# The bias of the first pair as a rank-one product: three banks filled by TensorE ahead of the data

## The chip, the cores and the metric

One core of one Trainium2 chip runs the whole program. The metric is the device time in microseconds (us) of one execution. The kernel before took 922.59 us, the median of three runs (922.33 to 923.38).

## The reference

`x` has 128 samples of 64 channels by 1024 columns. Each sample is first mixed by a 64x64 matrix that its condition picks out of 16; the result goes through a linear layer with a bias (`W`, `b`) and, beside it, through a low-rank product (`A`, `B`, weighted by `p_scores`) that is clamped against the linear part by row norms.

```python
cond = jnp.einsum('bct,bcd->bdt', x, cond_w[itok])          # 64 x 64 per sample
z = jnp.einsum('bsd,od->bso', cond, W) + b
u = jnp.einsum('bsd,edr->ebsr', cond, A)
m = jnp.einsum('ebsr,ero,e->bso', u, Bm, p_scores)
gamma = jnp.minimum(0.5 * norm(z) / (norm(m) + 1e-6), 1.0)  # norms over the last axis
out = x + z + gamma * m
```

## The kernel before

Two samples fill the 128 partitions and make a tile; there are 64 tiles in 32 pairs (tile r = 0 and r = 1 of a pair). For each tile TensorE mixes the channels by a block-diagonal `mixer` (plain float32 matmuls, `mix`, line 888) into PSUM, ScalarE and VectorE split the result into a high and a low part (`y_hi`, `y_lo`), and TensorE multiplies the parts with the high and low parts of `W` in three passes (`product`, line 901). `W` is cut into four 512x512 blocks W11, W12, W21, W22. Pairs 1 to 31 save products by a Strassen-like scheme, which needs sums of the blocks (T1 to T4, made by VectorE in pair 0) and sums of the tiles' halves (S1 to S4). Pair 0 doesn't: it does all eight block products plainly (`plain`) while the weights still arrive. Its results stand in four banks: z11 in `b_ps`, z21 in `a_ps`, z12 in `c_ps` and z22 in half of `m_ps`. `plain_done` counts them (5 for z11, 6 for z21, 7 for z12, 8 for z22).

Every engine works through its own list in the order of the code, and all waits are semaphores written by hand; no scheduler moves anything. What the change and the prediction touch:

- TensorE's opening: once a tile of zeros is set, `WARM` = 8 bf16 matmuls of 512 columns (line 982) into `u_ps`; then `mix` of tile 0 into `mix_ps` when `x_loaded[0]` and `mixer_loaded[0]` are there, `mix` of tile 1 into `m_ps`, and the plain products.
- ScalarE's opening: it issues the load of the first chunk of W11 (line 504), loads its table (line 506, which releases GpSimd's load of tile 1, line 380), and issues two of the four loads of mixer blocks (lines 509 and 510); SyncE issues the other two (lines 277 and 278).
- SyncE loads the bias, spread over 128 partitions, as the last of the constants (line 287).
- VectorE in pair 0 adds the bias while it takes z11 (line 764), z21 (772), z12 (778) and z22 (784) out of PSUM. Between them stand the making of T3, T1, T2 and T4 (lines 609, 616, 623 and 630), the sum and the low part of `u` (676 and 681), and the low parts of the next pair's `y` (649).
- ScalarE in pair 0, after splitting the weights: `b_hi` (526), the square of z11 (464), a copy of half of `u_ps` (450), `u_hi` (455), then for pair 1 high parts and copies (430 and 436), the square of z12 (471), and high parts of T4 and T2 (425).
- Four waits of TensorE behind it: `up(1)` of pair 0 (line 960) waits for z22; the second product into `b_ps` of pair 1 for VectorE's line 746; the product with S3 for VectorE's line 714; and the mix of tile 5 for VectorE's line 649.

Of the kernel before, what the change touches and what calls it, by code (L numbers as in the profile page):

```python
# [5 lines left out]
def conditioned_clamped_low_rank_linear_kernel(  # L6
# [26 lines left out]
    ALU = mybir.AluOpType  # L33
# [13 lines left out]
    WARM = 8  # L47
    STEPS = PAIRS // 2
    CLAMP, EPS = 0.5, 1e-6
    W11, W21, W22, T1, T2, T3, T4 = range(7)  # L50
    W12 = T4
# [13 lines left out]
    with ctx:  # L65
# [6 lines left out]
        def sem(name):  # L72
            return ctx.enter_context(nc.semaphore(name))
# [16 lines left out]
        bias = sb("bias", [P, 3, H], fp32)  # L90
# [8 lines left out]
        s23 = sb("s23", [P, 2, HC, P], fp32)  # L99
# [19 lines left out]
        idle = squares[:, lo]  # L119
        raw11 = w_hi_raw[:, T1, :, :]  # L120
# [28 lines left out]
        bias_loaded = sem("bias_loaded")  # L149
        idle_set = sem("idle_set")  # L150
# [83 lines left out]
        def y_part(tile, r, h):  # L234
            return tile[:, h * HC:(h + 1) * HC, r * P:(r + 1) * P]
# [23 lines left out]
        def _(sp):  # L259
# [26 lines left out]
            sp.dma_start(b_raw, bm.rearrange("e r o -> (e r) o")).then_inc(bm_loaded, 16)  # L286
            sp.dma_start(bias[:, 0:2, :], b.rearrange("(o h n) -> o h n", o=1, h=2).to_broadcast([P, 2, H])
# [121 lines left out]
        def _(act):  # L409
# [35 lines left out]
            def copy_u(p, first):  # L445

                act.wait_ge(u_done, p + 1)
                if not first:
                    act.wait_ge(m_done[0], p)
                nc.scalar.copy(u_raw[:, :], u_ps[:, 2 * P:4 * P]).then_inc(u_copied, 1)  # L450

            def split_u(p):

                act.wait_ge(u_summed, p + 1)
                nc.scalar.copy(u_hi[:, :], u_raw[:, :]).then_inc(u_hi_ready, 1)

            def square_z11(p, par, opening):

                act.wait_ge(z11_ready, p + 1)
                if not opening:  # L460
                    act.wait_ge(z12_squared, p)
                    act.wait_ge(m_squared[1], p)
                    act.wait_ge(z0_sum_ready, p)
                nc.scalar.activation(squares[:, lo], z0[:, par, lo], ACT.Square,  # L464
                                     accum_out=z11_sq).then_inc(z11_squared, 1)
# [37 lines left out]

            act.dma_start(raw11[:, 0, :], w_blocks[W11][0]).then_inc(w_loaded[W11][0], 16)
# [21 lines left out]
            nc.scalar.copy(b_hi[:, :], b_raw).then_inc(b_hi_ready, 1)  # L526
            square_z11(0, 0, True)
            copy_u(0, True)
            split_u(0)
# [69 lines left out]
        def _(dve):  # L599
# [147 lines left out]

            nc.vector.memset(mixer[:, :, :], 0.0).then_inc(mixer_zeroed, 1)
# [14 lines left out]
            dve.wait_ge(plain_done, 5)  # L763
            nc.vector.tensor_tensor(z0[:, 0, lo], b_ps[:, :], bias[:, 0, :], ALU.add).then_inc(z11_ready, 1)
# [6 lines left out]
            dve.wait_ge(plain_done, 6)  # L771
            nc.vector.tensor_tensor(z1[:, lo], a_ps[:, :], bias[:, 0, :], ALU.add).then_inc(z21_ready, 1)
# [4 lines left out]
            dve.wait_ge(plain_done, 7)  # L777
            nc.vector.tensor_tensor(z0[:, 0, up_], c_ps[:, :], bias[:, 1, :], ALU.add).then_inc(z12_ready, 1)
# [105 lines left out]
        def _(pe):  # L884
# [30 lines left out]
            def plain(bank, r, h, n):  # L915

                product(bank, y_part(y_hi, r, h), y_part(y_lo, r, h), n, h == 0, h == 1, r == 0, True
                        ).then_inc(plain_done, 1)
# [62 lines left out]
            for _ in range(WARM):  # L981
                nc.tensor.matmul(u_ps[:, :], idle[:, 0:P], idle, start=True, stop=True)
            pe.wait_ge(x_loaded[0], 16)
# [10 lines left out]
            for r, bank in ((0, c_ps[:, :]), (1, m_ps[:, lo])):  # L994
                plain(bank, r, 0, W12)
# [13 lines left out]
            plain(m_ps[:, lo], 1, 1, W22)  # L1009
# [104 lines left out]
```

## Time and profile before

| what | value |
|---|---|
| median of 3 runs | 922.59 us |
| time of the profiled execution | 922.25 us |
| its span | 920.3 us |
| mean granted TensorE clock | 0.998 |
| busy: TensorE matmul, weight load | 909.4 us (99%), 772.5 us (84%) |
| busy: VectorE, ScalarE, GpSimd | 589.7 us (64%), 367.6 us (40%), 321.3 us (35%) |
| chain that ended last | TensorE 92%, VectorE 4%, the rest under 2% each |

The chain of waits is on TensorE nearly all the time. Its busy time counts a matmul from its start to the modelled end of its results, so one matmul that follows another closely overlaps it; how far apart two of them start is the better price.

### The profile page before, as it was taken

What the parts mean: (1) busy time and instruction counts of PE and PEld (TensorE: products, weight loads), DVE (VectorE), ACT (ScalarE), POOL (GpSimd) and SP (SyncE); (2) the same over time, 40 slices, a digit from 0 to 9 for tenths busy, and PEclk for the clock granted to TensorE, in tenths of its full rate; (3) what the DMA queues carried; (4) which work ended last, traced back from release to release, by engine and by line L of the source; (5) the groups of instructions that cost most, each with busy time, mean ns of one, the idle gap of its engine ahead of it and who ended that gap; (6) DMA issues with size and microseconds to landing.
All of it is one profiled execution on the core that took longest, in us unless ns stands there. A gap on an engine that the chain in (4) does not pass through costs nothing.

```text
span 920.3 us, 14732 instructions
## 1 busy us (share of the span) xinstructions
PE 909.4 (99%) x4628; PEld 772.5 (84%) x4628; DVE 589.7 (64%) x930; ACT 367.6 (40%) x727; POOL 321.3 (35%) x318
## 2 busy tenths in 40 slices
PE   8999999999999999999999999999999999999997
PEld 6878888888888888888888888888888888888885
DVE  6996666556665666665576656666655757566665
ACT  6653343334334333433343343334333433433342
POOL 0024443234433244332344322443323443224432
PEclk9999999999999999999999999999999999999999
DMA  8212221122221222211222212222112222122211
GB/s 300 74 70 95 72 95 57 60 94 94 71 92 40 78 94 71 94 51 66 94 94 71 88 39 84 94 71 94 47 70 94 94 71 83 37 91 94 73 47 68
DMA packets 32744, 75.16 MB, mean 82 GB/s; under 512 B 12761, under 2 KB 13786, under 8 KB 32730
## 3 DMA queue, kind: packets, MB, share of 16 engines
q1 hardware_dynamic: 32138, 73.91, 22.8%
q10 hardware_dynamic: 448, 0.56, 0.2%
q0 software_dynamic: 144, 0.52, 0.1%
q8 instruction: 7, 0.11, 0.1%
q14 instruction: 7, 0.06, 0.0%
HBM read 41.42 MB, written 33.55 MB: 81 GB/s over the span
## 4 chain that ended last, share of the span: by engine, by line
PE 92%; DVE 4%; issue 1%; SPq 1%; DMA 1%; ACT 0%; POOL 0%; DVEq 0%; POOLq 0%
PE b_ps L901 35%; PE c_ps L901 18%; PE mix_ps L888 11%; PE m_ps L960 9%; PE a_ps L901 9%; PE u_ps L941 6%; PE u_ps L945 3%; DMA a_lo_raw<-in_L_ffn_A_dram 1%; DVE w_lo L640 1%; SPq L271 1%; DVE s_lo L670 0%; DVE y L649 0%; DVE w_lo_raw L616 0%; DVE w_hi_raw L630 0%; DVE w_lo_raw L623 0%
## 5 line engine op out<-in xcount | busy, mean ns | idle before, releaser
L430 ACT CAST y<-mix_ps 128x512 fp32r<-128x512 f32 x126 | 74.4, 591 | 298.5 <-PE mix_ps L888 298.5
L368 POOL TENSOR_TENSOR stats<-stats 128x1 f32<-128x1 f32 x32 | 17.8, 556 | 456.9 <-ACT squares L483 456.9
L901 PE MATMUL b_ps<-w_hi,y 128*128 128x512 f32 x512 | 168.2, 389 | 0.3 <-DVE z L746 0.3
L670 DVE TENSOR_TENSOR s_lo<-s,s_hi 128x512 fp32r<-128x512 f32 x124 | 135.7, 1114 | 4.2
L888 PEld LDWEIGHTS mix_ps<-mixer,x_in 128*128 128x128 f32 x1008 | 121.9, 191 | 7.6 <-issue 2.9
L888 PE MATMUL mix_ps<-mixer,x_in 128*128 128x128 f32 x1008 | 122.8, 275 | 1.3 <-DMA mixer<-in_L_cond_weights_dram 0.9
L443 ACT CAST s_hi<-s 128x512 fp32r<-128x512 f32 x124 | 76.6, 618 | 115.6 <-POOL s L342 93.4
L354 POOL TENSOR_TENSOR z<-z,x_in 128x512 f32<-128x512 f32 x61 | 79.2, 1299 | 113.7 <-ACT squares L464 113.7
L901 PEld LDWEIGHTS b_ps<-w_hi,y 128*128 128x128 f32 x512 | 96.1, 188 | 20.6 <-DVE z L746 0.7
L649 DVE TENSOR_TENSOR y<-mix_ps,y 128x512 fp32r<-128x512 f32 x126 | 86.4, 687 | 41.5 <-ACT s L436 39.5
L901 PE MATMUL b_ps<-w_lo,y 128*128 128x512 f32 x256 | 99.6, 389 | 0.0
L901 PE MATMUL c_ps<-w_hi,s_hi 128*128 128x512 f32 x248 | 99.1, 400 | 0.0
L901 PE MATMUL b_ps<-w_hi,s_hi 128*128 128x512 f32 x248 | 96.6, 390 | 0.3 <-DVE z L714 0.3
L901 PE MATMUL c_ps<-w_lo,s_hi 128*128 128x512 f32 x248 | 96.7, 390 | 0.0
L901 PE MATMUL c_ps<-w_hi,s_lo 128*128 128x512 f32 x248 | 96.6, 389 | 0.0
L901 PE MATMUL b_ps<-w_hi,s_lo 128*128 128x512 f32 x248 | 96.5, 389 | 0.0
L901 PE MATMUL b_ps<-w_lo,s_hi 128*128 128x512 f32 x248 | 96.5, 389 | 0.0
L720 DVE TENSOR_TENSOR z<-b_ps,z 128x512 f32<-128x512 f32 x31 | 21.4, 692 | 106.1 <-PE b_ps L901 106.1
L901 PE MATMUL a_ps<-w_hi,y 128*128 128x512 f32 x264 | 86.6, 389 | 0.0
L348 POOL TENSOR_TENSOR z<-z,x_in 128x1024 f32<-128x1024 f32 x30 | 72.2, 2408 | 0.0
L941 PE MATMUL u_ps<-y,a_hi 128*128 128x512 f32 x256 | 69.3, 392 | 0.0
L741 DVE TENSOR_TENSOR z<-a_ps,bias 128x512 f32<-128x512 f32 x31 | 21.4, 691 | 57.7 <-PE a_ps L901 57.7
(119 smaller groups left out, 1568.5 us busy)
## 6 DMA issues: line engine op xcount, KB each, us to landing
x_in<-in_x_dram SPq DMA_DIRECT2D x63, 512.0 KB, 3.7
out_dram<-z SPq DMA_DIRECT2D x62, 512.0 KB, 2.8
w_lo_raw<-in_L_ffn_W_dram SPq DMA_DIRECT2D x8, 256.0 KB, 6.3
mixer<-in_L_cond_weights_dram SPq DMA_DIRECT2D x126, 16.0 KB, 2.1
w_hi_raw<-in_L_ffn_W_dram SPq DMA_DIRECT2D x7, 256.0 KB, 6.2
out_dram<-z SPq DMA_DIRECT2D x3, 256.0 KB, 2.0
x_in<-in_x_dram POOLq DMA_DIRECT2D x1, 512.0 KB, 4.0
a_lo_raw<-in_L_ffn_A_dram SPq DMA_DIRECT2D x1, 512.0 KB, 8.1
```

The lines of the kernel that those rows point to most:

```text
L348: nc.gpsimd.tensor_tensor(z1[:, :], z1[:, :], x_in[:, slot, :], ALU.add).then_inc(residual1_ready, 1)
L354: nc.gpsimd.tensor_tensor(z0[:, par, cols], z0[:, par, cols], x_in[:, 2 * par, cols], ALU.add).then_inc(residual0_ready, 1)
L430: nc.scalar.copy(y_part(y_hi, r, h), source(h)).then_inc(y_hi_ready, 1)
L443: nc.scalar.copy(s_hi[:, n, :, :], s_raw(n)).then_inc(s_hi_ready, 1)
L649: nc.vector.tensor_tensor(y_part(y_lo, r, h), source(h), y_part(y_hi, r, h).bitcast(fp32), ALU.subtract).then_inc(y_lo_ready, 1)
L670: nc.vector.tensor_tensor(s_lo[:, n, :, :], s_raw(n), s_hi[:, n, :, :].bitcast(fp32), ALU.subtract).then_inc(s_lo_ready, 1)
L720: nc.vector.tensor_tensor(z1[:, up_], b_ps[:, :], z0[:, par, up_], ALU.add).then_inc(u3_ready, 1)
L888: made = nc.tensor.matmul(source(h)[:, k, :], x_in[:, slot, (h * HC + k) * P:(h * HC + k + 1) * P], mixer[:, r, :], start=True, stop=True)
L901: summed = nc.tensor.matmul(bank, left[:, k, :], right[:, n, k, :], start=(start and k == 0 and i == 0), stop=(stop and k == HC - 1 and i ...
L941: return nc.tensor.matmul(u_ps[:, :], a_hi[:, k, :], y[:, k, :, :], start=(k == 0), stop=(k == KC - 1))
L945: nc.tensor.matmul(u_ps[:, 0:2 * P], a_lo[:, k, :], y[:, k, 0, :], start=False, stop=False)
L960: summed = nc.tensor.matmul(m[:, c], left[:, part], right[:, c], start=(n == 0), stop=(n == 2))
```

## The change

TensorE writes the bias into the three banks `b_ps`, `a_ps` and `c_ps` before the data is there: a matmul of a row of ones (1 partition by 128) with a row of the bias (1 by 512) puts the same row on all 128 partitions. Pair 0's products into these banks no longer begin with a cleared bank but add to it; ScalarE copies z11, z21 and z12 out, where VectorE added the bias. z22 (in `m_ps`) is handled as before. Five of the eight warm-up matmuls go. ScalarE's queue issues a small load of the bias (one partition) as its first act; SyncE's load of the spread bias, which writes over that row, waits until the three matmuls are through. VectorE sets the ones in a part of `s23` that is free then.

```diff
-    WARM = 8
+    WARM = 3
+        ones = s23[0:1, 0, 0, :]
 @sync
+            sp.wait_ge(bias_spread, 3)
             sp.dma_start(bias[:, 0:2, :], b.rearrange("(o h n) -> o h n", o=1, h=2).to_broadcast([P, 2, H])
                          ).then_inc(bias_loaded, 16)
 @scalar
+            act.dma_start(bias[0:1, 0:2, :], b.rearrange("(o h n) -> o h n", o=1, h=2)).then_inc(bias_row_loaded, 16)
             act.dma_start(raw11[:, 0, :], w_blocks[W11][0]).then_inc(w_loaded[W11][0], 16)
...
             nc.scalar.copy(b_hi[:, :], b_raw).then_inc(b_hi_ready, 1)
+            act.wait_ge(plain_done, 5)
+            nc.scalar.copy(z0[:, 0, lo], b_ps[:, :]).then_inc(z11_ready, 1)
             square_z11(0, 0, True)
+            act.wait_ge(plain_done, 6)
+            nc.scalar.copy(z1[:, lo], a_ps[:, :]).then_inc(z21_ready, 1)
             copy_u(0, True)
+            act.wait_ge(plain_done, 7)
+            nc.scalar.copy(z0[:, 0, up_], c_ps[:, :]).then_inc(z12_ready, 1)
             split_u(0)
 @vector
+            nc.vector.memset(ones, 1.0).then_inc(ones_set, 1)
             nc.vector.memset(mixer[:, :, :], 0.0).then_inc(mixer_zeroed, 1)
...
-            dve.wait_ge(plain_done, 5)
-            nc.vector.tensor_tensor(z0[:, 0, lo], b_ps[:, :], bias[:, 0, :], ALU.add).then_inc(z11_ready, 1)
...
-            dve.wait_ge(plain_done, 6)
-            nc.vector.tensor_tensor(z1[:, lo], a_ps[:, :], bias[:, 0, :], ALU.add).then_inc(z21_ready, 1)
...
-            dve.wait_ge(plain_done, 7)
-            nc.vector.tensor_tensor(z0[:, 0, up_], c_ps[:, :], bias[:, 1, :], ALU.add).then_inc(z12_ready, 1)
 @tensor
-            def plain(bank, r, h, n):
-                product(bank, y_part(y_hi, r, h), y_part(y_lo, r, h), n, h == 0, h == 1, r == 0, True
+            def plain(bank, r, h, n, on_bias=True):
+                product(bank, y_part(y_hi, r, h), y_part(y_lo, r, h), n, h == 0 and not on_bias, h == 1, r == 0, True
                         ).then_inc(plain_done, 1)
...
             for _ in range(WARM):
                 nc.tensor.matmul(u_ps[:, :], idle[:, 0:P], idle, start=True, stop=True)
+            pe.wait_ge(ones_set, 1)
+            pe.wait_ge(bias_row_loaded, 16)
+            for bank, o in ((b_ps, 0), (a_ps, 0), (c_ps, 1)):
+                nc.tensor.matmul(bank[:, :], ones, bias[0:1, o, :], start=True, stop=False).then_inc(bias_spread, 1)
             pe.wait_ge(x_loaded[0], 16)
```

On TensorE, at the start of its list, before:

```order
1 L982 MATMUL u_ps<-squares 128x512 [waits idle_set]
2 L982 MATMUL u_ps<-squares 128x512 x7
3 L888 MATMUL mix_ps<-mixer,x_in 128x128 [waits mixer_loaded0,x_loaded0]
4 L888 MATMUL mix_ps<-mixer,x_in 128x128 x7
5 L888 MATMUL m_ps<-mixer,x_in 128x128 [waits mixer_loaded1,x1_loaded]
```

and of the change (its line numbers are some higher; `s` is the tile with the ones):

```order
1 L989 MATMUL u_ps<-squares 128x512 [waits idle_set]
2 L989 MATMUL u_ps<-squares 128x512 x2
3 L994 MATMUL b_ps<-bias,s 128x512 [waits bias_row_loaded,ones_set]
4 L994 MATMUL a_ps<-bias,s 128x512
5 L994 MATMUL c_ps<-bias,s 128x512
6 L895 MATMUL mix_ps<-mixer,x_in 128x128 [waits mixer_loaded0,x_loaded0]
7 L895 MATMUL mix_ps<-mixer,x_in 128x128 x7
```

Three float32 matmuls of 512 columns stand where five bf16 ones stood, and they wait for a load.

On VectorE, from the making of T3 to that of T4 in pair 0, before:

```order
10 L609 TENSOR_TENSOR w_lo_raw<-w_lo_raw 128x1024 x2
11 L764 TENSOR_TENSOR z<-b_ps,bias 128x512 [waits plain_done,bias_loaded]
12 L766 TENSOR_TENSOR b_lo<-b_lo_raw,b_hi 128x1024 [waits b_hi_ready]
13 L616 TENSOR_TENSOR w_lo_raw<-w_lo_raw,w_hi_raw 128x1024 [waits w_lo_ready,t3_made] x2
14 L769 TENSOR_TENSOR bias<-bias 128x512
15 L772 TENSOR_TENSOR z<-a_ps,bias 128x512 [waits plain_done]
16 L623 TENSOR_TENSOR w_lo_raw<-w_lo_raw 128x1024 [waits w_lo_ready,t1_made]
17 L676 TENSOR_TENSOR u_raw<-u_ps,u_raw 128x256 [waits u_copied]
18 L623 TENSOR_TENSOR w_lo_raw<-w_lo_raw 128x1024 [waits w_lo_ready,t1_made]
19 L681 TENSOR_TENSOR u_lo<-u_raw,u_hi 128x256 [waits u_hi_ready]
20 L778 TENSOR_TENSOR z<-c_ps,bias 128x512 [waits plain_done]
21 L630 TENSOR_TENSOR w_hi_raw<-w_hi_raw,w_lo_raw 128x1024 [waits w_lo_ready,t2_made]
```

and of the change:

```order
11 L621 TENSOR_TENSOR w_lo_raw<-w_lo_raw 128x1024 x2
12 L777 TENSOR_TENSOR b_lo<-b_lo_raw,b_hi 128x1024 [waits b_hi_ready,bias_loaded]
13 L628 TENSOR_TENSOR w_lo_raw<-w_lo_raw,w_hi_raw 128x1024 [waits w_lo_ready,t3_made] x2
14 L780 TENSOR_TENSOR bias<-bias 128x512
15 L635 TENSOR_TENSOR w_lo_raw<-w_lo_raw 128x1024 [waits w_lo_ready,t1_made]
16 L688 TENSOR_TENSOR u_raw<-u_ps,u_raw 128x256 [waits u_copied]
17 L635 TENSOR_TENSOR w_lo_raw<-w_lo_raw 128x1024 [waits w_lo_ready,t1_made]
18 L693 TENSOR_TENSOR u_lo<-u_raw,u_hi 128x256 [waits u_hi_ready]
19 L642 TENSOR_TENSOR w_hi_raw<-w_hi_raw,w_lo_raw 128x1024 [waits w_lo_ready,t2_made]
```

Three additions of 128x512 are gone, two ahead of `u_lo` and one behind it.

On ScalarE, of the change, from `b_hi` to the first high part of pair 1; lines 534, 537 and 540 are new, and the other rows are in their order of before:

```order
33 L532 CAST b_hi<-b_lo_raw 128x1024 [waits bm_scaled]
34 L534 COPY z<-b_ps 128x512 [waits plain_done]
35 L469 ACTIVATE squares,stats<-z 128x512 [waits z11_ready]
36 L537 COPY z<-a_ps 128x512 [waits plain_done]
37 L455 COPY u_raw<-u_ps 128x256 [waits u_done]
38 L540 COPY z<-c_ps 128x512 [waits plain_done]
39 L460 CAST u_hi<-u_raw 128x256 [waits u_summed]
40 L435 CAST y<-mix_ps 128x4x128 [waits mix_done]
```

The copy of z12 stands ahead of `u_hi`.

## Rows read from the trace of the kernel before

**Rows 1.** Page, busy time of the whole span

```profile
PE 909.4 (99%) x4628; PEld 772.5 (84%) x4628; DVE 589.7 (64%) x930; ACT 367.6 (40%) x727; POOL 321.3 (35%) x318
```

**Rows 2.** Waits of TensorE: who waited, for whom, total, times, longest

```profile
PE mix_ps L888 <- DMA mixer<-in_L_cond_weights_dram: 0.9, 1, 0.9
PE mix_ps L888 <- DVE y L649: 0.4, 1, 0.4
PE b_ps L901 <- DVE z L714: 0.3, 1, 0.3
PE m_ps L960 <- DVE z L784: 0.3, 1, 0.3
PE b_ps L901 <- DVE z L746: 0.3, 1, 0.3
```

**Rows 3.** Windows: length, busy PE, PEld, DVE, ACT, POOL, granted clock, DMA

```profile
1.70:5.40 3.70, 3.59 (x8) 1.04 (x8) 0.00 (x0) 1.51 (x3) 0.71 (x2) 1.00 0.70 250
...
66.00:892.00 826.00, 826.00 (x4228) 705.65 (x4227) 517.42 (x826) 321.84 (x649) 305.53 (x298) 1.00 0.22 76
```

**Rows 4.** Timeline, TensorE's opening: start us, busy us, what

```profile
1.73 3.59 PE L982 MATMUL u_ps<-squares 128*128 128x512 bf16 x8 [1.73 <-POOL squares L375]
...
6.18 2.02 PE L888 MATMUL mix_ps<-mixer,x_in 128*128 128x128 f32 x16 [0.86 <-DMA mixer<-in_L_cond_weights_dram]
...
8.25 1.86 PEld L888 LDWEIGHTS m_ps<-mixer,x_in 128*128 128x128 f32 x16 [0.24 <-issue]
```

**Rows 5.** Timeline, TensorE, a mix between products at 32 us

```profile
32.02 1.95 PE L888 MATMUL mix_ps<-mixer,x_in 128*128 128x128 f32 x16
33.72 0.48 PE L901 MATMUL m_ps<-w_hi,y 128*128 128x512 f32 x1
```

**Rows 6.** Timeline, the queues' opening

```profile
0.74 0.40 ACTq L504 DMA_DIRECT2D w_hi_raw<-in_L_ffn_W_dram  x1
...
2.97 0.58 ACTq L509 DMA_DIRECT2D mixer<-in_L_cond_weights_dram  x1
...
3.29 0.71 POOL L380 DMA_DIRECT2D x_in<-in_x_dram  x1 [1.58 <-ACT stats L506]
...
4.40 0.47 SPq L278 DMA_DIRECT2D mixer<-in_L_cond_weights_dram  x1
```

**Rows 7.** Chain of waits, a small load in the opening

```profile
0.72 1.27 DMA cond_ids<-in_itok_B_dram
```

**Rows 8.** Issue to landing of lines 504, 278 and 380, in this order

```profile
DMA to landing us min/median/max: 2.8/2.8/2.8
DMA to landing us min/median/max: 3.8/3.8/3.8
DMA to landing us min/median/max: 4.0/4.0/4.0
```

**Rows 9.** Waits of VectorE from 22 to 66 us, the whole answer

```profile
DVE a_lo L759 <- ACT a_hi L521: 1.5, 1, 1.5
```

**Rows 10.** Timeline of VectorE, pair 0

```profile
33.75 0.42 DVE L681 TENSOR_TENSOR u_lo<-u_raw,u_hi 128x256 fp32r<-128x256 f32 x1
...
34.09 0.68 DVE L778 TENSOR_TENSOR z<-c_ps,bias 128x512 f32<-128x512 f32 x1
...
34.69 1.22 DVE L630 TENSOR_TENSOR w_hi_raw<-w_hi_raw,w_lo_raw 128x1024 f32<-128x1024 f32 x1
```

**Rows 11.** Timeline of TensorE and ScalarE around `u_hi`

```profile
31.79 0.39 PE L901 MATMUL c_ps<-w_hi,y 128*128 128x512 f32 x1
...
32.73 0.41 ACT L455 CAST u_hi<-u_raw 128x256 fp32r<-128x256 f32 x1 [2.87 <-DVE u_raw L676]
...
33.59 0.59 ACT L436 COPY s<-mix_ps 128x512 f32<-128x512 f32 x1
...
34.06 0.60 ACT L430 CAST y<-mix_ps 128x512 fp32r<-128x512 f32 x1
```

**Rows 12.** Timeline, the last wait of TensorE for VectorE

```profile
64.89 2.02 PE L888 MATMUL mix_ps<-mixer,x_in 128*128 128x128 f32 x16 [0.43 <-DVE y L649]
```

More of the change, by code:

```diff
@@ L149, in conditioned_clamped_low_rank_linear_kernel @@
         bias_loaded = sem("bias_loaded")
+        bias_row_loaded = sem("bias_row_loaded")
+        ones_set = sem("ones_set")
+        bias_spread = sem("bias_spread")
         idle_set = sem("idle_set")
@@ L993, in _ @@
                 plain(bank, r, 0, W11)
-            for r, bank in ((0, c_ps[:, :]), (1, m_ps[:, lo])):
-                plain(bank, r, 0, W12)
+            plain(c_ps[:, :], 0, 0, W12)
+            plain(m_ps[:, lo], 1, 0, W12, False)
             for r, bank in ((0, b_ps[:, :]), (1, a_ps[:, :])):
@@ L1008, in _ @@
                 mix(0, 2, h)
-            plain(m_ps[:, lo], 1, 1, W22)
+            plain(m_ps[:, lo], 1, 1, W22, False)
             mix_next_1(0, 0, 0)
```

## The prediction

> **What bounds the kernel now.** I read the busy times first: TensorE's matmuls fill 99% of the span [rows 1]. The windows then show where the other 1% is. From 66 to 892 us TensorE is busy for all of 826.00 us [rows 3], so nothing that pair 0 saves or loses there is made up or lost again: a time by which TensorE is earlier or later at 66 us goes through to the end, one for one. The waits of TensorE are five that bear on this change: 0.9 us for the mixer blocks in the opening, and four of 0.3 to 0.4 us for VectorE, all before 66 us [rows 2]; the last of them is the mix at 64.89 [rows 12]. VectorE in turn waits only once from 22 to 66 us, 1.5 us ahead of `a_lo`, which stands before all that the change touches in pair 0 [rows 9]: behind it VectorE is a full queue, and the four waits are waits for that queue. So two numbers decide: how much later TensorE gets through its opening (call it d), and how much earlier VectorE's queue runs at 64 us.
>
> **The opening: warm-up and spread.** The eight bf16 matmuls take 3.59 us from 1.73 [rows 4]. 512 columns at 1.2 GHz are 0.427 us; eight are 3.42, and the 0.17 left is the tail that every matmul row has (0.39 for 512 columns [rows 11], of which 0.213 at 2.4 GHz). So all eight ran at the lower clock, although the window's granted clock says 1.00 [rows 3]; I trust the spacing. Three of them end at 1.73 + 3 x 0.427 = 3.01.
>
> The row of the bias is issued at 0.74, where the load of W11 was [rows 6]. No row shows this load; the nearest are a 0.5 KB one that lands 1.27 us after its issue [rows 7] and the 256 KB one with 2.8 [rows 8]. That gives 2.0 to 3.5; it is nearer to the small one, so I take it that it doesn't hold TensorE: start at 3.05, by the upper bound 3.54.
>
> The price of one spreading matmul: float32 matmuls are two records each (a mix has 8 in the code and 16 in the trace). Sixteen records of 128 columns start and end within 33.72 - 32.02 = 1.70 us [rows 5], 0.106 each, which is 2 x 128 columns at 2.4 GHz. If the records pass their columns twice, one of 512 columns is 0.427 us at 2.4 GHz and 0.853 at 1.2. The other reading is that loading the weights sets the 0.106 and the columns go through once: then 0.213 and 0.427. I take the first: 6 records x 0.427 or 0.853. The Trainium skill, FP8 and Floating Point Precision, section TensorE Precision Notes, says that true float32 takes four passes through the array: two records of two passes, with which the 1.70 us agree. By the other reading the result would be that of the second case below.
>
> When does the clock rise? Before, the eighth matmul still streamed slowly, until 5.15, and the mix at 6.18 was fast (2.02 us for 16 records, against 3.4 at 1.2 GHz) [rows 4]. So it rose between 5.15 and 6.18, and I take the middle, 5.65. With it: (5.65 - 3.05) / 0.853 = 3.05 records slow, 2.95 x 0.427 = 1.26 us fast, end at 6.91. The first mix then starts 6.91 - 6.18 = 0.73 us later. Ends of this: rise at 5.15 and start at 3.0 give 6.64 (+0.46); rise at 6.18 and start at 3.54 give 7.42 (+1.24).
>
> Part of it comes back at once. The second mix began at 8.25 after 0.24 us in which nothing was issued [rows 4]: line 278's mixer block, issued at 4.40, took 3.8 us, to 8.20 [rows 6, 8]. SyncE's queue isn't moved, so a later TensorE no longer meets this wait: d = 0.73 - 0.25 = 0.5 (0.2 to 1.0).
>
> ScalarE's own queue is 0.40 us later by the new issue [rows 6]: line 509 (2.97), its table, and with the table GpSimd's load of tile 1 (3.29 to 3.7, landing 4.0 later at 7.7 [rows 6, 8], before the second mix wants it). TensorE, busy until 6.9, hides these; were the spread short, they would cost 0 to 0.4. The memset of ones (128 elements on one partition) stands ahead of the mixer's, for which the loads of lines 277 and 509 wait; they wait for the conditions as well, until 1.99 [rows 7], and were issued at 2.97 and later. No row shows it; it is far under the 0.6 us for which a 128x512 addition holds VectorE [rows 10], so it is hidden. SyncE's new wait stands where the queue comes at 16.5 us, long after the spread: nothing. Accumulating onto a bank instead of clearing it changes no column: nothing, and no row suggests a gain.
>
> **Pair 0: three additions leave VectorE, three copies go to ScalarE.** An addition of 128x512 holds VectorE for 34.69 - 34.09 = 0.60 us [rows 10]; three are 1.8 us, and with a full queue all behind would be 1.8 us earlier. But `u_lo` stands among them. It waits for `u_hi`, and ScalarE now makes `u_hi` behind the copy of z12, which waits for the last product into `c_ps`. Its last matmul ended at 31.79 + 0.39 = 32.18 [rows 11], now 32.68; copy at 32.73, `u_hi` one pitch later (34.06 - 33.59 = 0.47 [rows 11]) at 33.20, ending 33.61, `u_lo` at 33.7. Before, it was at 33.75 [rows 10]. So the 1.2 us won ahead of it are spent waiting there, and only the third addition, right behind it, is a gain: T4 starts at 34.04 instead of 34.69, VectorE 0.6 us earlier. This depends on d: VectorE's lead is 1.1 - d.
>
> Behind that, ScalarE's high parts come some 0.5 us later than before (the first at 33.6), which the making of T4 (1.22 [rows 10]) covers; the squares of z11 and z21 have slack, for their users stand behind line 784.
>
> **The four waits.** VectorE is 0.6 us earlier at each. TensorE starts 0.5 us late, loses that against the first (z22) and the second (line 746), whose waits it no longer has, and then meets VectorE's queue again: at the product with S3 and at the mix of 64.89 it is as early as VectorE is. The waits don't vanish, they move by 0.6 us. Sum: VectorE's three additions -1.8, the new wait for `u_hi` +1.2, net -0.6 us at 66 us; the later opening is already paid out of the waits. The profiled execution had a span of 920.3 and a time of 922.25 us: that gives 919.7 and 921.65. The median of the runs lies 0.34 above that execution, so I forecast 922.59 - 0.6 = **922.0 us**. By the bounds of d the gain is 0.1 to 0.9.
>
> **The other cases.** A change of 0.2% is 1.85 us, about what a measurement of this kernel can tell from none; below 920.75 I call it faster, above 924.45 slower.
>
> - Cheap spread (8%). If a record passes its columns once, the spread ends by 5.6 even at the lower clock, d is about 0, the lead of VectorE is 1.1 us, and the time 921.5. For it: weight loading could set the 0.106. Against: 16 records match two passes to the nanosecond. Even with the whole 1.8 us it would be 920.8.
> - The lead doesn't come through (10%). The clock rises later, or ScalarE, which is 0.5 us later at the high parts, keeps VectorE waiting again at the low parts of `y`. With all six records slow the spread ends at 3.05 + 5.12 = 8.17, d is 1.7, and the net +0.6: 922.6 to 923.4. For it: the rise is known only to 1 us.
> - Slower: the spread doesn't count as work (12%). Its matmuls use one of 128 partitions of the array. If they don't raise the clock, the spread ends at 8.17, the mix starts slow, and the rise comes, if as long after the start of the work as before (at least 5.15 - 1.73 = 3.4), at 11.6 or later: 3.4 / 0.213 = 16 records slow, 16 fast (1.7): 13.3 instead of 10.0 for the first product, d = 3.3, and the net 3.3 - 1.1 = +2.2: 924.8 us, and more if the rise is a microsecond later. It decides where d passes 3.0. For it: nothing in the trace shows such a matmul. Against: the rise came after a stretch with no more than these weights and zeros going through. The Trainium skill, TensorE: Matmul & The Clock Gate, Part 4, says that transposes on TensorE are not counted as busy in the same way and leave the clock low; no run here shows such a kind. If it held for one-partition matmuls the time would be that 924.8.
>
> **Chances.** The forecast 70%, the others as given. Faster by over 0.2%: 3% (none of the cases gives it; it is what I leave for a price that I misread). Slower: 11%. Same: 86%. The range is 921.0 to 923.8: it holds the forecast, the cheap spread and the lead lost, and leaves the slow clock out.
>
> **What would show it.** In the profile after: three float32 matmuls in six records from about 3.0, with the first slow (0.85 apart) and the last fast (0.43); first mix at 6.6 to 7.4, without a wait for the mixer; no unissued 0.24 us ahead of the second mix; `u_lo` near 33.7 with VectorE now waiting for `u_hi` some 1 us; T4's making at 34.0; no wait of TensorE for z22 and line 746; waits for lines 714 and 649 still there, the mix of 64.89 at 64.3; 66 to 890 us full. I am wrong if the mix of 64.89 moves by over 1 us either way, if the mix after the spread is slow, or if TensorE waits anywhere else.

## The result, and the profile after

The change takes 925.23 us (median of 12 runs) against 922.82 for the kernel before (12 runs): a ratio of 1.0027, 95% interval 1.002 to 1.0035. It is slower, by 2.4 us, and my 922.0 and range to 923.8 missed it. One of the twelve runs took 1629 us at a mean granted clock of 0.68 and doesn't enter the ratio; the other eleven lie between 924.83 and 926.17. The case to which I gave 12%, at 924.8 us, is what happened. The profiled execution of the change has a span of 922.9 us where before had 920.3.

TensorE's opening in the profile of the change (timeline; start us, busy us, what):

```profile
1.73 1.46 PE L989 MATMUL u_ps<-squares 128*128 128x512 bf16 x3 [1.73 <-POOL squares L380]
...
3.12 2.07 PE L994 MATMUL b_ps<-bias,s 1*128 1x512 f32 x2
...
4.99 1.91 PE L994 MATMUL a_ps<-bias,s 1*128 1x512 f32 x2
4.99 0.33 PEld L994 LDWEIGHTS a_ps<-bias,s 1*128 1x128 f32 x1 [0.52 <-issue]
...
5.84 0.33 PEld L994 LDWEIGHTS c_ps<-bias,s 1*128 1x128 f32 x1 [0.52 <-issue]
...
6.70 1.91 PE L994 MATMUL c_ps<-bias,s 1*128 1x512 f32 x2
...
8.54 3.74 PE L895 MATMUL mix_ps<-mixer,x_in 128*128 128x128 f32 x16
...
12.11 1.95 PE L895 MATMUL m_ps<-mixer,x_in 128*128 128x128 f32 x16
13.82 0.48 PE L908 MATMUL b_ps<-w_hi,y 128*128 128x512 f32 x1
```

The weight loads at 4.99 and 5.84 and the matmuls at 4.99 and 6.70 give the pace of the records: 0.85 us each, 1024 columns at 1.2 GHz. All six are that slow. The first mix starts at 8.54 instead of 6.18 (+2.36), and runs slow itself: 3.57 us until the second mix, where before had 2.11 (8.29 - 6.18, the start in the timeline of before; +1.46). The second mix is fast. The first product starts at 13.82; before it was 10.06. Together d = 3.76 us where I had forecast 0.5. The granted clock in the windows says 1.00 here too:

```profile
1.70:5.40 3.70, 3.67 (x6) 1.45 (x7) 0.00 (x0) 1.79 (x3) 0.71 (x2) 1.00 0.72 230
```

The waits that TensorE still has behind its opening, those of VectorE from 14 to 70 us, then `u_lo` and T4 (VectorE) and the mix of tile 5:

```profile
PE mix_ps L895 <- DVE y L661: 0.4, 1, 0.4
PE b_ps L908 <- DVE z L726: 0.3, 1, 0.3
```

```profile
DVE u_lo L693 <- ACT u_hi L460: 1.7, 1, 1.7
DVE u_raw L688 <- ACT u_raw L455: 1.2, 1, 1.2
```

```profile
36.87 0.42 DVE L693 TENSOR_TENSOR u_lo<-u_raw,u_hi 128x256 fp32r<-128x256 f32 x1 [1.68 <-ACT u_hi L460]
37.21 1.22 DVE L642 TENSOR_TENSOR w_hi_raw<-w_hi_raw,w_lo_raw 128x1024 f32<-128x1024 f32 x1
...
67.47 2.02 PE L895 MATMUL mix_ps<-mixer,x_in 128*128 128x128 f32 x16 [0.43 <-DVE y L661]
```

Of the five waits of [rows 2] the mixer's, z22's and line 746's are gone; those for lines 714 (726 now) and 649 (661) are as long as before. The mix of tile 5 starts 67.47 - 64.89 = 2.58 us later [rows 12], which is the 2.6 us of the spans: nothing behind it matters. So of the 3.76 us lost in the opening, 1.18 did not arrive.

Two questions follow. Why did the clock stay low, and does the move of the additions give back those 1.18 us?

### The profile page after: what moved, and what is told of

It reads as the page before. It is cut to its first block, busy times and chain, and to the rows that moved or that the text cites. A ratio compares the mean times of both kernels' runs of the same rounds, so it can differ in the third digit from the quotient of the medians.

```text
span 922.9 us, 14737 instructions
## 1 busy us (share of the span) xinstructions
PE 913.5 (99%) x4629; PEld 775.3 (84%) x4629; DVE 587.1 (64%) x928; ACT 367.6 (40%) x730; POOL 321.2 (35%) x318
## 4 chain that ended last, share of the span: by engine, by line
PE 95%; DVE 3%; issue 1%; POOL 0%; ACT 0%; DVEq 0%; POOLq 0%
PE b_ps L908 36%; PE c_ps L908 18%; PE mix_ps L895 12%; PE a_ps L908 9%; PE m_ps L967 9%; PE u_ps L948 6%; PE u_ps L952 3%; DVE w_lo L652 1%; DVE s_lo L682 0%; PE m_ps L908 0%; PE b_ps L994 0%; DVE y L661 0%; PE m_ps L895 0%; PE a_ps L994 0%; PE c_ps L994 0%
## 5 line engine op out<-in xcount | busy, mean ns | idle before, releaser
L732 DVE TENSOR_TENSOR z<-b_ps,z 128x512 f32<-128x512 f32 x31 | 21.4, 692 | 106.1 <-PE b_ps L908 106.1
L908 PEld LDWEIGHTS a_ps<-w_hi,y 128*128 128x128 f32 x264 | 49.6, 188 | 10.3
```

The lines of the kernel that those rows point to most:

```text
L732: nc.vector.tensor_tensor(z1[:, up_], b_ps[:, :], z0[:, par, up_], ALU.add).then_inc(u3_ready, 1)
L908: summed = nc.tensor.matmul(bank, left[:, k, :], right[:, n, k, :], start=(start and k == 0 and i == 0), stop=(stop and k == HC - 1 and i ...
```

## Experiments

### Does a matmul of one partition raise the clock?

Three kernels built on the one before, and the change with more warm-up.

```diff
 e1_warm_one_row, on before
-                nc.tensor.matmul(u_ps[:, :], idle[:, 0:P], idle, start=True, stop=True)
+                nc.tensor.matmul(u_ps[:, :], squares[0:1, 0:P], squares[0:1, lo], start=True, stop=True)
```

> The kernel before, whose eight warm-up matmuls read one partition of the zeros in place of 128; same columns, same number, same type. Theory A (matmuls that use one partition of the array don't raise TensorE's clock): the mix at 6.18 runs at 1.2 GHz, 16 records 0.213 us apart instead of 0.117, and the first product starts at 11.5 to 13.5 instead of 10.06; the time is 1 to 2.5 us over that of before. Theory B (float32 matmuls, or their spacing, don't count, the partitions play no part): the mix is fast as before, first product at 10.06, time of before within 0.3 us. Theory C (eight of the bf16 matmuls are needed and the three of the change were too few): as B, fast.

```diff
 e2_float32_all_rows, on before
-    WARM = 8
+    WARM = 3
+            idle32 = squares[:, :].bitcast(fp32)
+            for _ in range(3):
+                nc.tensor.matmul(u_ps[:, :], idle32[:, 0:P], idle32, start=True, stop=True)
```

> The kernel before with three bf16 warm-up matmuls and behind them three float32 ones of 512 columns over all 128 partitions of zeros (as long as the spread of the bias, but no bias and no wait). Theory A: they count; the clock rises between 5.1 and 6.2 us, the last records are 0.43 apart, the first mix starts at 6.6 to 7.2 and is fast, first product at 10.3 to 11.0; time +0.2 to +1 us over before. Theory B: all six records 0.853 apart, first mix at 8.2 to 8.5 and slow, first product at 13.8 as in the change. Theory C: as B.

```diff
 e3_three_warm, on before
-    WARM = 8
+    WARM = 3
```

> The kernel before with three warm-up matmuls in place of eight and nothing behind them. Theories A and C: from 3.0 us on nothing counts, as in the change, so the mix at 6.18 is slow (0.213), the clock rises at 9.5 to 12 and the first product starts at 11.5 to 13.5; time +1 to +3 us. If the clock had risen in the change by its own (a rise that falls at a fixed time, whatever TensorE does), the mix would be fast and the time that of before.

```diff
 e4_eight_warm_and_spread, on the change
-    WARM = 3
+    WARM = 8
```

> The change with eight warm-up matmuls in place of three; the spread of the bias starts at 5.15 instead of 3.12. Theory A: the eight have raised the clock by 6.2, so of the six records one or two are slow and the rest 0.43 apart; end at 7.9 to 8.3, first mix fast, first product at 11.6 to 12.0 instead of 13.82, time 922.8 to 923.8. Theory B, the same if a high clock outlives the float32 records. If one-partition matmuls count as idle and let the clock fall again at once, the mix is slow and the time 925 or more.

The openings of TensorE, first of the eight one-partition warm-ups:

```profile
1.73 3.59 PE L982 MATMUL u_ps<-squares 1*128 1x512 bf16 x8 [1.73 <-POOL squares L375]
5.84 3.75 PE L888 MATMUL mix_ps<-mixer,x_in 128*128 128x128 f32 x16 [0.53 <-DMA mixer<-in_L_cond_weights_dram]
9.39 2.09 PE L888 MATMUL m_ps<-mixer,x_in 128*128 128x128 f32 x16
11.23 0.48 PE L901 MATMUL b_ps<-w_hi,y 128*128 128x512 f32 x1
```

then of the float32 ones over all partitions:

```profile
2.98 4.56 PE L985 MATMUL u_ps<-squares 128*128 128x512 f32 x6
7.37 1.95 PE L888 MATMUL mix_ps<-mixer,x_in 128*128 128x128 f32 x16
9.16 1.95 PE L888 MATMUL m_ps<-mixer,x_in 128*128 128x128 f32 x16
10.86 0.48 PE L901 MATMUL b_ps<-w_hi,y 128*128 128x512 f32 x1
```

and of the change with eight warm-ups:

```profile
5.25 2.07 PE L994 MATMUL b_ps<-bias,s 1*128 1x512 f32 x2
7.12 1.91 PE L994 MATMUL a_ps<-bias,s 1*128 1x512 f32 x2
8.83 1.91 PE L994 MATMUL c_ps<-bias,s 1*128 1x512 f32 x2
10.67 3.60 PE L895 MATMUL mix_ps<-mixer,x_in 128*128 128x128 f32 x16
...
15.81 0.48 PE L908 MATMUL b_ps<-w_hi,y 128*128 128x512 f32 x1
```

In e1, with the same columns and times but one partition instead of 128, the mix is slow (3.55 us from one mix to the next), where before had it fast. In e2 float32 matmuls over all partitions, of zeros, raise the clock on the way: six records take 4.4 us instead of 5.4, and the mix behind them is fast (1.79 from one to the next). So float32 records of this length don't by themselves keep the clock low (against theory B), and three bf16 warm-ups are not too few (against C). What is left is the one partition (A).

Each of the two is one execution, and e1 by itself proves little: in e10 (below) the mix is slow behind eight full-width warm-ups too. The repeated runs carry more. The profiles of the change (924.83 us or more in eleven runs) and of e8 below, which has the same opening (924.59 or more in nine), have a time that is 857.5 to 857.6 us more than the start of the mix of tile 5, and that start 53.7 us behind the first product. By this estimate the first product came at 13.3 us or later in all twenty; with a fast first mix it would have come near 12.1 (8.54 + 2 x 1.78), and earlier still had the clock risen within the spread. And in all six profiles with one-partition matmuls ahead of the first mix (the change, e1, e4, e7, e8, e11) that mix is slow, while in the seven with full-width work alone and more than three matmuls it is fast in five (before, e2, e6, e9, e12), partly slow in e5 and slow in e10. e2 and the change still differ in the values (zeros, against ones and the bias) and in the banks written; e1, with zeros into one bank, is the only kernel that sets this apart.

With nothing behind three warm-ups (e3) the first product started at 12.35, with the spread behind them at 13.82: as far as the clock goes the spread was no better than idling, and it moved the first mix from 5.96 to 8.54. Eight warm-ups ahead of it (e4) did not help: I expected one or two slow records, and all six are slow and the mix too, first product 15.81, time 927.12 us. So the clock had not risen by 10.67 although the eight were through at 5.2, as in before, where a mix at 6.18 was fast. The one-partition records behind them are what differs, or the luck of that run: with eight full warm-ups and nothing behind them the first mix was also partly slow in e5 and slow in e10. One run can't tell these apart.

The times of e1 and e3, 922.43 and 923.39 (922.36 for before on the same chip), are 0.1 and 1.0 us over it, where I expected 1 to 2.5 and 1 to 3: e1 misses, e3 is at the lower bound. e1's first product (11.23) is a little ahead of the expected 11.5 to 13.5 as well, and e2's first mix (7.37) a little behind 6.6 to 7.2. The first products of e1 and e3 are 1.17 and 2.29 us late, and less than half of it arrives at the end. Theory A had the clock right, and I had overlooked what absorbs a late opening.

### Where do the additions' 1.8 us go?

The opening of the change put alone into before (spread done, its result overwritten, VectorE adds the bias as before); and the change with the copy of z12 behind `u_hi`.

```diff
 e8_opening_alone, on before
-    WARM = 8
+    WARM = 3
...
+            sp.wait_ge(bias_spread, 3)               # ahead of the load of the spread bias
...
+            act.dma_start(bias[0:1, 0:2, :], b.rearrange("(o h n) -> o h n", o=1, h=2)).then_inc(bias_row_loaded, 16)
...
+            nc.vector.memset(ones, 1.0).then_inc(ones_set, 1)
...
+            pe.wait_ge(ones_set, 1)
+            pe.wait_ge(bias_row_loaded, 16)
+            for bank, o in ((b_ps, 0), (a_ps, 0), (c_ps, 1)):
+                nc.tensor.matmul(bank[:, :], ones, bias[0:1, o, :], start=True, stop=True).then_inc(bias_spread, 1)
```

> The opening of the change alone: three warm-up matmuls, the load of the bias row, the one-partition spread in float32. Its result isn't used: the products clear their banks as before and VectorE adds the bias as before. Theory D (the moved additions bring nothing here, since VectorE waits for what TensorE, late by the opening, lets ScalarE copy of pair 1): first product at 13.8 as in the change, mix of tile 5 at 67.3 to 67.6 as there (67.47), time 924.9 to 925.5. Theory E (the opening costs 3.7 us and the moved additions give 1.1 back): mix of tile 5 at 68.3 to 68.7, time 926.0 to 926.5.

```diff
 e7_z12_behind_u_hi, on the change
-            act.wait_ge(plain_done, 7)
-            nc.scalar.copy(z0[:, 0, up_], c_ps[:, :]).then_inc(z12_ready, 1)
             split_u(0)
+            act.wait_ge(plain_done, 7)
+            nc.scalar.copy(z0[:, 0, up_], c_ps[:, :]).then_inc(z12_ready, 1)
```

> The change with ScalarE's copy of z12 behind u_hi instead of ahead of it. Theory D (what holds VectorE is the copy of the second half of pair 1's tile, for which the low part of y waits): u_lo at about 35.1 instead of 36.87, the first part of T4 at 35.5 instead of 37.21, but the second part at 39.5 to 39.7 and the mix of tile 5 at 67.3 to 67.6, unmoved. Theory F (the wait for u_hi is what holds it, as I had worked out): the second part of T4 0.5 to 1.2 us earlier and the mix of tile 5 at 66.3 to 67.0.

The opening alone: 925.03 us (9 runs), ratio 1.0025 (1.0015 to 1.0035), the same as the whole change. Its first product was at 14.29 (the clock rose in the second mix), and the mix of tile 5 at 67.98, 53.69 us behind it. In the change it is 67.47 - 13.82 = 53.65, in e7 and e11, which have the same opening and the moved additions, 53.69. The three moved additions bring nothing here: theory E falls.

With z12 behind `u_hi` (925.14 us) `u_lo` comes at 35.18 and T4 at 35.52, 1.7 us earlier than in the change, and then VectorE waits for the copies of pair 1 instead. Its timeline and waits:

```profile
35.18 0.42 DVE L693 TENSOR_TENSOR u_lo<-u_raw,u_hi 128x256 fp32r<-128x256 f32 x1
35.52 1.22 DVE L642 TENSOR_TENSOR w_hi_raw<-w_hi_raw,w_lo_raw 128x1024 f32<-128x1024 f32 x1
...
38.09 0.69 DVE L661 TENSOR_TENSOR y<-mix_ps,y 128x512 fp32r<-128x512 f32 x1 [1.36 <-ACT s L441]
...
39.07 0.69 DVE L661 TENSOR_TENSOR y<-mix_ps,y 128x512 fp32r<-128x512 f32 x1 [0.29 <-ACT s L441]
...
39.68 1.22 DVE L642 TENSOR_TENSOR w_hi_raw<-w_hi_raw,w_lo_raw 128x1024 f32<-128x1024 f32 x1
...
67.56 2.02 PE L895 MATMUL mix_ps<-mixer,x_in 128*128 128x128 f32 x16 [0.43 <-DVE y L661]
```

The second half of T4 is at 39.68 (39.60 in the change) and the mix of tile 5 at 67.56. The wait for `u_hi`, on which I had built my sum, is not what holds VectorE (theory F falls): the low part of `y` needs ScalarE's copy of the mixed tile of pair 1, and that comes when TensorE has mixed it, a fixed time behind the first product.

The start of `a_lo` in before, and the operation to which the text comes back at the end:

```profile
22.53 1.23 DVE L759 TENSOR_TENSOR a_lo<-a_lo_raw,a_hi 128x1024 fp32r<-128x1024 f32 x1 [1.47 <-ACT a_hi L521]
...
54.52 2.39 DVE L670 TENSOR_TENSOR s_lo<-s,s_hi 128x512 fp32r<-128x512 f32 x2
```

The kernels side by side, P the start of the first product, A the start of `a_lo`, M that of the mix of tile 5, all from the timelines:

| kernel | P | A | M | M - P | M - A |
|---|---|---|---|---|---|
| before | 10.06 | 22.53 | 64.89 | 54.83 | 42.36 |
| e1 one-partition warm-up | 11.23 | 22.74 | 65.10 | 53.87 | 42.36 |
| e2 float32 warm-up | 10.86 | 23.32 | 65.68 | 54.82 | 42.36 |
| e3 three warm-ups | 12.35 | 23.14 | 66.04 | 53.69 | 42.90 |
| the change | 13.82 | 23.76 | 67.47 | 53.65 | 43.71 |
| e4 change, eight warm-ups | 15.81 | 25.76 | 69.50 | 53.69 | 43.74 |
| e7 z12 behind `u_hi` | 13.87 | 23.80 | 67.56 | 53.69 | 43.76 |
| e8 opening alone | 14.29 | 23.81 | 67.98 | 53.69 | 44.17 |

Up to here M is the later of P + 53.69 and A + 42.36. In before the second decides, as in e1 and e2, whose P differ and whose M - A is the same 42.36: the load of A lands at 21.4 us, VectorE waits for it, and from there its queue is full to 64. TensorE's opening had 64.89 - 53.69 - 10.06 = 1.14 us to spare. That is what absorbed e1's late product, and what absorbed 1.2 of the 3.76 us of the change. The additions lie on the other of the two paths.

### Is there a version that gains?

If the rule holds, the additions pay once TensorE's opening is cheap. The spread as float32r is one record per matmul (ScalarE rounds the row and the ones; the bias is rounded to float32r for three of pair 0's four blocks), placed behind the first mix, with eight warm-ups. SyncE's load of the spread bias now waits for ScalarE's rounding of the row.

```diff
 e5_cheap_spread_z12_late and e6_cheap_spread, on the change
-    WARM = 3
+    WARM = 8
...
-        ones = s23[0:1, 0, 0, :]
+        ones = s_hi[0:1, 0, 0, :]
+        bias_row = b_hi[0:1, :]
...
+            nc.scalar.copy(bias_row, bias[0:1, 0:2, :].rearrange("p h n -> p (h n)")).then_inc(bias_row_split, 1)
+            act.wait_ge(raw_ones_set, 1)
+            nc.scalar.activation(ones, s23[0:1, 0, 0, :], ACT.Copy).then_inc(ones_set, 1)
...
-            for bank, o in ((b_ps, 0), (a_ps, 0), (c_ps, 1)):
-                nc.tensor.matmul(bank[:, :], ones, bias[0:1, o, :], start=True, stop=False).then_inc(bias_spread, 1)
             pe.wait_ge(x_loaded[0], 16)
             pe.wait_ge(mixer_loaded[0], 16 * PER)
             for h in range(2):
                 mix(0, 0, h)
+            pe.wait_ge(ones_set, 1)
+            pe.wait_ge(bias_row_split, 1)
+            for bank, o in ((b_ps, lo), (a_ps, lo), (c_ps, up_)):
+                nc.tensor.matmul(bank[:, :], ones, bias_row[:, o], start=True, stop=False)
 e5 alone: ScalarE's copy of z12 behind split_u(0), as in e7
```

> The change with a cheap spread: eight warm-up matmuls as before, and the spread behind the first mix, at the high clock, as float32r with one record per matmul (ScalarE rounds the row and the ones first; the bias is rounded to float32r for three of pair 0's four blocks). ScalarE's copy of z12 stands behind u_hi. If the price is three records of 0.21 to 0.23 less the 0.25 us for which TensorE stood ahead of the second mix, the first product starts 0.3 to 0.5 us later than before (10.4 to 10.6 where the load of A lands as before). Theory D: the mix of tile 5 is 0.7 to 0.8 us earlier than before relative to the landing of A, time 921.7 to 922.2. Theory F: with z12 late all 1.8 us of the three additions come through, mix 1.6 to 1.8 us earlier, time 920.7 to 921.2. Theory G (the mix of tile 5 is set by the landing of A alone, the additions don't matter): as before.

> As the cheap spread, but with ScalarE's copy of z12 ahead of u_hi, as in the change. Theory D: mix of tile 5 0.6 to 0.7 us earlier than before, within 0.2 us of the version with z12 late. Theory F: 0.6 to 0.7 us earlier, but the version with z12 late gains 1 us more.

Of e6, the opening of TensorE, ScalarE's high parts of W11, a stall in the first product, and the mix of tile 5:

```profile
5.59 2.02 PE L902 MATMUL mix_ps<-mixer,x_in 128*128 128x128 f32 x16 [0.38 <-DMA mixer<-in_L_cond_weights_dram]
7.54 0.49 PE L1004 MATMUL b_ps<-b_hi,s_hi 1*128 1x512 f32 x1
7.88 0.39 PE L1004 MATMUL a_ps<-b_hi,s_hi 1*128 1x512 f32 x1
8.12 0.38 PE L1004 MATMUL c_ps<-b_hi,s_hi 1*128 1x512 f32 x1
8.43 2.05 PE L902 MATMUL m_ps<-mixer,x_in 128*128 128x128 f32 x16
10.24 0.48 PE L915 MATMUL b_ps<-w_hi,y 128*128 128x512 f32 x1
...
10.58 1.26 ACT L422 CAST w_hi<-w_hi_raw 128x512 fp32r<-128x512 f32 x2 [0.96 <-DMA w_hi_raw<-in_L_ffn_W_dram]
...
12.07 0.47 PE L915 MATMUL b_ps<-w_hi,y 128*128 128x512 f32 x1 [0.19 <-DVE w_lo L623]
...
64.42 2.02 PE L902 MATMUL mix_ps<-mixer,x_in 128*128 128x128 f32 x16 [0.43 <-DVE y L668]
```

Here the load of A was late (`a_lo` at 23.84), and M - A is 64.42 - 23.84 = 40.58, 1.78 less than the 42.36 of before. The path from A can't be longer than that, so it is shorter by at least 1.78: this is the 3 x 0.60 of the additions, in full, and with z12 ahead of `u_hi`. M - P is 54.18 in both, so P decided in both. It is 0.49 over 53.69, of which 0.45 lie in the first product: it stalls for a low part of `W`, behind a chunk of W11 for which ScalarE waits until 10.58 in e6 and 12.06 in e5 (its three in before start at 8.82 without a wait). It is a load that is late, and whether the new work in the opening makes it so isn't shown; the landing of A, too, is latest in these two. In e5 the first mix was partly slow as well (P = 11.03), and M = 65.21. Of the expectations, theory D gave 0.6 to 0.8 us relative to A's landing, and measured are 0.92 and 1.78; F expected z12 late to be the better by 1 us; M - P is the same in both, and e6 has the whole gain without it. Times: 922.38 us (10 runs), ratio 0.9993 (0.9983 to 1.0002) for e5, 922.02 for the single run of e6.

```diff
 e9_spread_in_gaps, on e5
-    WARM = 8
+    WARM = 9
...
+            act.wait_ge(plain_done, 1)               # ahead of b_hi, in whose place the rounded row stands
...
+            nc.tensor.matmul(b_ps[:, :], ones, bias_row[:, lo], start=True, stop=False)      # between the mixes
...
+            def spread_rest():                                                             # ahead of chunk 2 of the first product
+                for bank, o in ((a_ps, lo), (c_ps, up_)):
+                    nc.tensor.matmul(bank[:, :], ones, bias_row[:, o], start=True, stop=False)
```

> The cheap float32r spread with nine warm-up matmuls, the matmul into the first bank between the two mixes and those into the other two within the first product, where the last version had lost 0.2 to 0.5 us waiting for the low parts of W; ScalarE copies z12 behind u_hi. Theory D: first product at about 10.1 to 10.2, no stall in it, but 0.45 us of spread; by the rule the mix of tile 5 at 64.2 to 64.5, time 921.8 to 922.4, a gain of 0.3 to 0.8 us. Rival: one-partition matmuls in the middle of full ones let the clock fall; then the products behind them would be 0.43 apart instead of 0.23 and the time 923.5 or more.

It measured 922.38 us (11 runs), 0.9998 (0.9989 to 1.0007), P = 10.00, M = 64.52, without a low clock behind the one-partition matmuls. The first product took 3.68 us up to the start of the next, 0.84 more than the 2.84 of before (12.90 - 10.06), where I had allowed 0.45; P + 53.69 + 0.84 = 64.53 is its M. So M was just outside the expected 64.2 to 64.5 and no gain can be told from none.

The other path can be shortened without any spread: VectorE makes T3 while it waits for A.

```diff
 e10_t3_ahead_of_a_lo on before; e11_change_t3_ahead on the change
+            make_t3(0)
+            make_t3(1)
             dve.wait_ge(a_hi_ready, 1)
             nc.vector.tensor_tensor(a_lo[:, :, :], a_raw, a_hi[:, :, :].bitcast(fp32), ALU.subtract).then_inc(a_lo_ready, 1)
-            make_t3(0)
-            make_t3(1)
```

> The kernel before with one swap on VectorE: T3 is made ahead of a_lo, for which VectorE stood waiting 1.5 us (for the load of A) while it could have made T3. Theory D, as a rule: the mix of tile 5 starts at the later of (first product + 53.69) and (a_lo + 42.36); in before the second, 64.89. The swap takes about 1.5 us from the second, so the first decides: with the first product near 10.06 the mix starts at 63.7 to 64.0 and the time falls by 0.9 to 1.2 us (0.10 to 0.13%). If the first product starts late in that run (the clock rising later, as in two runs of this study), the gain is less by as much over 11.2. Theory H (TensorE's opening sets the end in before too): nothing moves, 922.6 to 922.9.

> The change with the same swap. Theory D: nothing, since the first product at 13.8 decides: mix of tile 5 at 67.4 to 67.6, time 925.0 to 925.4. Theory H and any theory by which VectorE's queue still decides: 1 to 1.5 us less.

On the change it did nothing, as the rule has it: 924.99 us, P = 13.71, M = 67.40, 53.69 apart. On before the result was 922.98 us (11 runs), 0.9998 (0.9989 to 1.0007), against the expected 0.10 to 0.13% less. The profile shows why in that execution:

```profile
1.73 3.60 PE L982 MATMUL u_ps<-squares 128*128 128x512 bf16 x8 [1.73 <-POOL squares L375]
6.97 3.68 PE L888 MATMUL mix_ps<-mixer,x_in 128*128 128x128 f32 x16 [1.65 <-DMA mixer<-in_L_cond_weights_dram]
10.49 1.95 PE L888 MATMUL m_ps<-mixer,x_in 128*128 128x128 f32 x16
12.19 0.48 PE L901 MATMUL b_ps<-w_hi,y 128*128 128x512 f32 x1
...
65.87 2.02 PE L888 MATMUL mix_ps<-mixer,x_in 128*128 128x128 f32 x16 [0.47 <-DVE y L649]
```

The same eight warm-ups as in before, and the mix slow, at 6.97: P = 12.19, M = P + 53.68. So in this execution P decides. The expectation named this case, but the rule was not put to the test by it. That P had decided in before too (theory H) doesn't fit its M - P of 54.83; the unmoved median alone would. The eleven times of e10 run from 921.35 to 923.70, five of them at 922.2 or less.

```diff
 e12_swap_and_eleven_warm, on e10
-    WARM = 8
+    WARM = 11
```

> The kernel before with T3 made ahead of a_lo and eleven full warm-up matmuls in place of eight. The swap alone gave two groups of times, 921.4 to 921.8 and 922.2 to 923.7; by theory D they are runs in which the clock rose ahead of the first mix and runs in which it rose within it. If so, full work up to 6.4 us, where TensorE now stands idle from 5.2, leaves the first group alone: first product at 10.0 to 10.7, mix of tile 5 at 63.7 to 64.4, all times within 921.2 to 922.2, median 921.5 to 921.9 (0.08 to 0.12% under before). Rival: the two groups come from the loads (the mixer blocks landed 0.8 us later in the profiled run of the swap), and they stay: times from 921.4 to 923.7, median as before.

```profile
1.73 4.12 PE L982 MATMUL u_ps<-squares 128*128 128x512 bf16 x11 [1.73 <-POOL squares L375]
5.87 2.02 PE L888 MATMUL mix_ps<-mixer,x_in 128*128 128x128 f32 x16
8.68 2.02 PE L888 MATMUL m_ps<-mixer,x_in 128*128 128x128 f32 x16 [0.78 <-DMA mixer<-in_L_cond_weights_dram]
10.45 0.47 PE L901 MATMUL b_ps<-w_hi,y 128*128 128x512 f32 x1
...
63.58 2.02 PE L888 MATMUL mix_ps<-mixer,x_in 128*128 128x128 f32 x16
```

This has the lowest median of all, 921.69 us against 922.67 (11 and 15 runs), and the group above 922.4 is gone; but the ratio on record is 0.9993 (it is not the ratio of the medians, 0.9989) with an interval of 0.9984 to 1.0002, so a gain isn't shown. Before spread from 921.3 to 923.7 in the same comparison. M is 63.58, 53.13 behind P, 0.56 less than the rule's 53.69. Two rows of VectorE and one of GpSimd say what the rule lacks:

```profile
25.55 0.69 DVE L764 TENSOR_TENSOR z<-b_ps,bias 128x512 f32<-128x512 f32 x1 [0.85 <-DMA bias<-in_L_ffn_b_dram]
...
53.93 4.38 POOL L354 TENSOR_TENSOR z<-z,x_in 128x512 f32<-128x512 f32 x1 [6.41 <-ACT squares L464]
...
54.14 1.29 DVE L670 TENSOR_TENSOR s_lo<-s,s_hi 128x512 fp32r<-128x512 f32 x2
```

First, with T3 out of the way VectorE meets the load of the bias, 0.85 us. Line 764 starts at 25.55, in before at 25.94, 0.39 earlier though A landed 0.34 later: the swap is worth 0.73 us here, and not the 1.5 on which the expectation of e10 was built. Second, VectorE's two low parts at line 670 take 1.29 us beside a GpSimd addition of 4.38; in the other thirteen profiles they take 2.38 or 2.39 beside one of 1.45, so the 42.36 and the 53.69 both have 1.1 us of this in them. From line 764 to M before has 38.95 us; 25.55 + 38.95 - 1.10, and 0.17 for a longer operation at line 640 (58.01), is 63.57. That gives M, and P + 53.69 less the same 0.93 is 63.21, so P didn't decide here. That M is 1.31 us ahead of before's with P 0.39 later fits theory D and not H.

So of these 1.31 us only 0.39 come from the earlier line 764; the meeting of VectorE and GpSimd at 54 us gives the rest, and no experiment here controls it. Whether the clock, the landings of x and the mixer blocks (from 5.6 to 7.0 us in these profiles) or this meeting of the two engines make the spread of the times stays open.

## Why the prediction was wrong, by its steps

- **Spread of the bias, pace of a record: right.** Two passes per record, 0.427 or 0.853 us; measured 0.85 at the low clock. The fast pace shows only in e2, in six records of 4.4 us. The row of the bias held nothing up (start 3.12 against 3.05).
- **"With it: (5.65 - 3.05) / 0.853 = 3.05 records slow, 2.95 x 0.427 = 1.26 us fast": this step failed.** I took the time at which the clock rose in before for a time of the kernel, though it depended on the full-width work from 1.73 to 5.15, five eighths of which the change removes, and I counted the one-partition records as if they were such work. Measured: six records slow, and the mix behind them. d is 3.76 and not 0.5. I had the mechanism as a case, with d = 3.3 and 924.8 us; its size was right (+2.2 against +2.4 in the medians), its 12% too little. The Trainium skill (TensorE: Matmul & The Clock Gate, Part 4) says of transposes that they don't count as busy in the same way; no run here has one, but the runs show a second kind of work of which that holds.
- **"Part of it comes back at once": right.** The 0.24 us ahead of the second mix are gone.
- **"The 1.2 us won ahead of it are spent waiting there": wrong in its reason.** The wait for `u_hi` is in the profile, 1.68 us, but taking it away moved nothing (e7). My lead "1.1 - d" has the right number by luck: 1.1 us is what TensorE's opening had to spare in before (1.14), which has nothing to do with the additions (e8). By that luck the slow case, 3.3 - 1.1, came so near the measured time.
- **"VectorE is a full queue": right, and read one step short.** The one wait that [rows 9] shows, 1.5 us for the load of A, was the start of the path that set the end. The additions do shorten it, by 1.78 us (e6) and not by 0.6. A gain behind it counts on that path alone, and only down to the other one.
- **The four waits:** I expected two to go and two to stay, and the same two went and stayed, but not for my reason: e8, in which VectorE still does all the additions, has the same two. **66 us to the end passes a shift on one for one:** 2.58 at 67 us, 2.6 in the span.

That the clock had a phase of its own was in reach as well: The Trainium skill (same page, Part 1) says that the point of the rise varies from run to run. By the runs here it does: with eight full warm-ups and nothing behind them the first mix was fast in before and in e6, partly slow in e5 and slow in e10. I had read one profile of before as the rule.

## What to carry to other kernels

Warm-up of TensorE is not replaced by just any work that keeps it busy: here one-partition matmuls kept it busy for 5.4 us and left the clock where idling left it. Before something is moved off a full engine, find what each of the paths to the next common wait starts from (here a load and TensorE's first product): work moved off one of them is worth at most the distance to the other, and a delay is free up to the same distance. A wait that shows up in a profile is not yet the one that decides; what comes next on the same engine may wait for something later still, as VectorE did for the bias once T3 was out of the way.

## What the runs showed of the hardware

- Matmuls over one partition, bf16 (eight, 3.4 us) or float32 (six records, 5.1 us), left the first mix behind them at 1.2 GHz in all six profiles that have them; work over 128 partitions, zeros as they were, had raised the clock by then in five of seven.
- The granted clock of the profile's windows said 1.00 in stretches where records came at half the pace (0.85 us for 1024 columns): in an opening the spacing has to be read instead.
- A one-partition float32r matmul of 512 columns took 0.24 to 0.34 us from start to start at the high clock (7.54, 7.88, 8.12); in e9, with one between the two mixes and two within the first product, the products behind them kept their 0.23.
- When GpSimd's addition of 128x512 (line 354) and VectorE's two low parts of 128x512 (line 670) met at 54 us, they took 1.45 and 2.39 us in thirteen profiles and 4.38 and 1.29 in one (e12): one or the other is stretched.
